# Softmax bands of a local-attention stage moved by DMA instead of ScalarE, and the softmax division moved from GpSimd to ScalarE

## The reference

```
shift_tokens(x):  second half of the features is taken from the token before
q, k, v = split(shift_tokens(x) @ Wqkv)            # 16 heads of 64
q, k = rotary(l2norm(q) * q_scale), rotary(l2norm(k) * k_scale)
# windows of 32 tokens; a token of window w sees windows w-1 and w, through a mask
attn = softmax(8 * q k^T);  x = x + (attn v) @ Wo
h = shift_tokens(x);  h = layernorm(h) * g + b
x = x + (a * gelu(gate)) @ W2 + b2     where a, gate = split(h @ W1 + b1)
```

## Time and profile before

| | us |
|---|---|
| three runs, median (lowest to highest) | 7142.1 (7134.1 to 7146.59) |
| the profiled execution, its own time | 7146.77 |
| its span, first to last instruction | 7144.5 |
| last stage, first to last division L1575 | 3055.2 to 7043.7 |

### The profile page before, as it was taken

How to read it: one execution, slowest core, us unless ns; L and a number is a source line. 1 busy time by engine, 2 the same in 40 slices (tenths; PEclk the granted TensorE clock), 3 DMA queues, 4 the chain that set the end, 5 groups by cost and what they waited for, 6 DMA issues and landing times. The chain is left out here.

```text
span 7144.5 us, 148393 instructions
## 1 busy us (share of the span) xinstructions
PE 5401.0 (76%) x55030; PEld 3273.5 (46%) x55030; DVE 4401.4 (62%) x5698; ACT 3887.7 (54%) x6333; POOL 3429.4 (48%) x1391
## 2 busy tenths in 40 slices
PE   4736777087594848578888888888888888888886
PEld 3524444022121212255555555555555555555554
DVE  4352111342333424488888888888888888888885
ACT  0002222022131213278888777887778778888884
POOL 0000000000000000188888888888888888888883
PEclk8658888588796869789999999999999999999997
DMA  0000000300101010000000000000000000000001
GB/s 17 0 7 20 27 27 27 50 2 12 16 0 27 1 27 0 35 22 7 6 7 28 6 6 13 21 7 6 12 22 7 6 27 6 7 7 12 7 7 28
DMA packets 79753, 102.01 MB, mean 14 GB/s; under 512 B 16344, under 2 KB 55138, under 8 KB 77934
## 3 DMA queue, kind: packets, MB, share of 16 engines
q1 hardware_dynamic: 79632, 100.41, 6.4%
HBM read 63.67 MB, written 11.53 MB: 11 GB/s over the span
## 5 line engine op out<-in xcount | busy, mean ns | idle before, releaser
L99 POOL TENSOR_TENSOR ln_post_rstd<-ln_post_var,neg_half 128x8 f32<-128x8 f32 x16 | 26.6, 1662 | 2922.8 <-DVE ln_post_var L80 2922.8
L1591 POOL TENSOR_TENSOR d_qk_swap<-d_qk_raw,d_rot 128x512 f32<-128x512 f32 x768 | 1389.0, 1838 | 67.4 <-ACT d_qk_raw L1299 40.4
L1598 POOL TENSOR_TENSOR d_rnorm<-d_sq_clip,neg_half 128x32 f32<-128x32 f32 x192 | 1232.4, 6419 | 271.6 <-DVE d_sq_clip L1466 271.6
L834 ACT ACTIVATE c_pt<-c_ps 128x512 f32<-128x512 f32 (+1 forms) x640 | 354.5, 555 | 1118.8 <-PE c_ps L752 1116.8
L1137 PE MATMUL d_ring<-d_wqkv,d_xin 128*128 (+1 forms) x1536 | 810.2, 665 | 174.3 <-ACT d_xin L1389 169.3
L866 DVE TENSOR_REDUCE c_mx<-c_ps 128x1 f32<-128x512 f32 (+3 forms) x768 | 416.8, 556 | 772.9 <-PE c_ps L737 768.9
L1449 DVE TENSOR_TENSOR d_qk_part<-d_qk_raw,d_rot 128x1024 f32<-128x1024 f32 x384 | 597.7, 1559 | 253.6 <-ACT d_qk_raw L1299 251.0
L1575 POOL TENSOR_TENSOR d_probs_n<-d_probs,d_prec 128x1024 f32<-128x1024 f32 x192 | 545.5, 2841 | 315.8 <-DVE d_prec L1491 315.8
L1299 ACT ACTIVATE d_qk_raw<-d_ring 128x512 f32<-128x512 f32 x768 | 435.8, 594 | 453.9 <-PE d_ring L1137 450.2
L766 PE MATMUL c_ps<-c_pt,c_vg 128*32 128x512 f32 (+3 forms) x1536 | 629.3, 507 | 4.7 <-DVE c_ots L871 4.7
L1137 PEld LDWEIGHTS d_ring<-d_wqkv,d_xin 128*128 128x128 f32 x1536 | 319.7, 216 | 560.0 <-issue 449.2
(11 more groups left out here) (259 smaller groups left out, 10498.5 us busy)
## 6 DMA issues: line engine op xcount, KB each, us to landing
d_v_prev<-d_v SPq DMA_DIRECT2D x192, 128.0 KB, 2.3
b_w<-in_L_ffn_w SPq DMA_DIRECT2D x64, 256.0 KB, 3.4
d_wqkv<-in_L_ffn_Wqkv SPq DMA_DIRECT2D x6, 1536.0 KB, 8.7
c_kp<-c_k_scratch SPq DMA_DIRECT2D x30, 256.0 KB
c_qp<-c_q_scratch SPq DMA_DIRECT2D x24, 256.0 KB
d_rot<-in_rot_base SPq DMA_DIRECT2D x6, 1024.0 KB, 6.4
c_k_scratch<-c_kparts SPq DMA_DIRECT2D x5, 768.0 KB, 5.2
c_q_scratch<-c_qparts SPq DMA_DIRECT2D x4, 768.0 KB, 3.6
```

What stands on the lines that cost most here:

```text
L1591: mm = eng.tensor_tensor(qk_swap[:, which, :, out:out + hd], qk_raw[:, which, :, src:src + hd], rot[:, bass.ds(par, 1), which, 1, bass.ds( ...
L1598: eng.tensor_tensor(rnorm[:, :], sq_clip[:, :], neg_half[:, 0:2 * HEADS], ALU.pow).then_inc(rn_ready, 1)
```

## The change

Five edits, all in the last stage.

1. The eight band copies go from ScalarE to SyncE's DMA queue: eight `dma_start` a slot, each 32 partitions x 512 numbers. The band tile becomes 128 x 4 windows x 16 heads x 32, so that each transfer writes one run per partition; the product with v reads it with a stride. `band_ready` counts 16 for each transfer, 128 a slot.
2. SyncE's slot now waits for `blocks_ready`, issues the eight transfers, then waits for `pv_ready` and issues the carry of `v_prev`.
3. The division of the probabilities goes from one GpSimd instruction to sixteen ScalarE instructions of 128 x 64, one per head, with the reciprocal as a scale operand read from `prec`.
4. Order on VectorE: the block transposes stand after the layer-norm and residual steps; in odd slots the row sums and reciprocal stand behind the scaling by the norms. Order on TensorE: `qk(2)` and `qk(3)` go ahead of the W2 product, `values` ahead of the variance product.
5. Order on ScalarE: the input copy `xin` goes ahead of the v copies; in even slots Gelu goes ahead of Exp, behind a one-column Gelu (`table_probe`).

```diff
-        band = [sb(f"band{p}", [P, HEADS, P]) for p in range(2)]
+        band = [sb(f"band{p}", [P, 4, HEADS, WIN]) for p in range(2)]
...
-                    eng.wait_ge(v_evac, 2 * (m + 1))
-                    eng.wait_ge(pv_ready, m + 1)
-                    eng.dma_start(v_prev[P - WIN:P, :], v_sb[p][P - WIN:P, :]).then_inc(v_carried, 16)
+                def slot(n, u, f, g):
+                    if f:
+                        eng.wait_ge(blocks_ready, n - 1)
+                        eng.sem_inc(passed, 1)
+                        if f == 2:
+                            eng.wait_ge(pv_ready, n - 3)
+                        for w in range(4):
+                            r = slice(32 * w, 32 * w + 32)
+                            eng.dma_start(band[u][r, w, :, :], own_t[r, :, :]).then_inc(band_ready, 16)
+                            to = band[u][32 * w - 32:32 * w, w, :, :] if w else band_prev[u][96:128, :, :]
+                            eng.dma_start(to, prev_t[r, :, :]).then_inc(band_ready, 16)
+                    if g:
+                        eng.wait_ge(pv_ready, n - 2)
+                        eng.dma_start(v_prev[P - WIN:P, :], v_sb[1 - u][P - WIN:P, :]).then_inc(v_carried, 16)
...
-                    if u == 0:
-                        if f:
-                            bands((0, 1))
+                    if f:
+                        eng.wait_ge(rec_ready, n - 1)
                         if g:
-                            attended()
-                        if f:
-                            bands((2, 3))
-                    elif f:
-                        bands((0, 1, 2, 3))
+                            eng.wait_ge(blocks_ready, n - 2)
+                        for h in range(HEADS):
+                            mm = eng.activation(probs_n[:, h, :], probs[:, h, :], ACT.Copy, scale=prec[:, h:h + 1])
+                        mm.then_inc(pn_ready, 1)
+                    if g and u == 0:
+                        attended()
...
-                    if f:
-                        eng.wait_ge(rec_ready, n - 1)
-                        if live(3):
-                            eng.wait_ge(blocks_ready, n - 2)
-                        eng.tensor_tensor(probs_n[:], probs[:], prec[:, :].unsqueeze(2).broadcast_to((P, HEADS, 2 * WIN)),
-                                          ALU.mult).then_inc(pn_ready, 1)
```

More of the change, by code:

```diff
@@ L1066, in _, with pairs, through @@
                 eng.wait_ge(zeroed, 1)
-                def carry(m, p):
-                    eng.wait_ge(v_evac, 2 * (m + 1))
-                    eng.wait_ge(pv_ready, m + 1)
-                    eng.dma_start(v_prev[P - WIN:P, :], v_sb[p][P - WIN:P, :]).then_inc(v_carried, 16)
-                def tiles(lo, hi, l):
+                def slot(n, u, f, g):
[12 more added lines that the diff above has]
+                        eng.dma_start(v_prev[P - WIN:P, :], v_sb[1 - u][P - WIN:P, :]).then_inc(v_carried, 16)
+                def pairs(lo, hi, l):
                     with eng.Fori(lo, hi) as k:
                         for u in range(2):
-                            carry(l * NT + k * 2 + u, u)
-                def turn_over(l):
+                            slot(l * NT + k * 2 + u, u, 2, True)
+                for n in range(4):
+                    slot(n, n % 2, int(n >= 2), n >= 3)
+                load(1, 1)
+                pairs(2, 16, 0)
+                def through(l, more):
+                    pairs(0, 2, l)
                     eng.wait_ge(wo_ready, (NT // 2) * l)
                     load_wo(l)
+                    pairs(2, 3, l)
                     eng.wait_ge(w1_ready, 3 * (NT // 2) * l)
@@ L1086, in turn_over @@
                     load_w2(l)
-                tiles(0, 3, 0)
-                load(1, 1)
-                tiles(3, 16, 0)
+                    if more:
+                        eng.wait_ge(x2_ready, (NT // 2) * l)
+                        load(l + 1, (l + 1) % 2)
+                    pairs(3, 16, l)
                 with eng.Fori(1, LAYERS - 1) as l:
[L1092 to L1101, removed]
+                    through(l, True)
+                through(LAYERS - 1, False)
+                slot(TILES, 0, 2, True)
+                slot(TILES + 1, 1, 2, True)
+                eng.wait_ge(v_carried, 16 * (TILES - 1))
                 for b in range(BATCH):
@@ L1179, in attended @@
                     def attended():
-                        eng.wait_ge(band_ready, n - 2)
+                        eng.wait_ge(band_ready, 128 * (n - 2))
                         eng.wait_ge(ot_ready, n - 3)
@@ L1189, in attended @@
                             r, at = place(h)
-                            eng.matmul(op[r:r + 64, h // 2, :], v_sb[1 - p][:, h * DH:(h + 1) * DH], band[1 - p][:, at, :],
+                            eng.matmul(op[r:r + 64, h // 2, :].rearrange("p (w t) -> p w t", t=WIN), v_sb[1 - p][:, h * DH:(h + 1) * DH], band[1 - p][:, :, at, :],
                                        start=(h % 8 < 2), stop=False, skip_group_check=True, tile_position=(0, r))
@@ L1203, in slot @@
                         qk(1)
+                    if a:
+                        qk(2)
+                        qk(3)
                     if late:
@@ L1209, in slot @@
                         mm.then_inc(w2_ready, 1)
-                    if a:
-                        qk(2)
-                        qk(3)
                     if s:
@@ L1238, in slot @@
                         attended()
+                    if s:
+                        par_v = eng.snap(parity(n - 1))
+                        values(0)
+                        values(1)
                     if odd:
@@ L1244, in slot @@
                         mm.then_inc(var_done, 1)
[L1245 to L1248, removed]
                     if even:
@@ L1316, in turned @@
                         eng.activation((qt[:, :, :], kt[:, :, WIN:])[c % 2][:, 4 * half:4 * half + 4, :], src, ACT.Copy).then_inc(t_evac, 1)
[L1318 to L1332, removed]
                     def attended():
@@ L1344, in values @@
                     def values():
+                        eng.wait_ge(v_ready, 2 * n)
+                        if live(-1):
+                            eng.activation(xin[1 - p][:, :], xs[:, bass.ds(eng.snap(column(n + 1)), P)], ACT.Copy).then_inc(xin_ready, 1)
                         for c in range(2):
@@ L1387, in slot @@
                         values()
-                    if live(-1):
+                    elif live(-1):
                         eng.activation(xin[1 - p][:, :], xs[:, bass.ds(eng.snap(column(n + 1)), P)], ACT.Copy).then_inc(xin_ready, 1)
-                    if s and u == 0:
-                        exponent()
                     if even:
+                        eng.activation(table_probe[:, :], keep[:, 0:1], ACT.Gelu)
                         par_f = eng.snap(parity(n - 6))
@@ L1397, in slot @@
                                            bias=b1[0:w, bass.ds(par_f, 1), 3 + c:4 + c].rearrange("p l c -> p (l c)")).then_inc(gelu_ready, 1)
+                    if s and u == 0:
+                        exponent()
                 run(eng, slot, layer_start)
@@ L1484, in slot, with total @@
                         par, i = eng.snap(parity(n)), eng.snap(n % TB)
-                    if f:
+                    def total():
                         eng.wait_ge(exp_ready, n - 1)
@@ L1491, in slot @@
                         eng.reciprocal(prec[:], psum_row[:]).then_inc(rec_ready, 1)
+                    if f and u == 0:
+                        total()
                     if late:
@@ L1505, in slot @@
                                           ALU.mult).then_inc(rope_ready, 1)
+                    if f and u == 1:
+                        total()
                     if a:
@@ L1517, in slot @@
                         cosine(1).then_inc(cos_done, 1)
-                    if f:
-                        blocks()
                     if even:
@@ L1535, in slot @@
                         mm.then_inc(x1_ready, 1)
+                    if f:
+                        blocks()
                     if u == 0 and a:
```

## The result

The changed kernel takes 7913.94 us (median of four runs, 7908.4 to 7919.42) against 7144.35 for the kernel before: ratio 1.1078, 95% interval 1.1059 to 1.1098. That is 770 us slower. The forecast was 7680, the range 7400 to 8010.

A forecast was written before the change was run, and what follows sets the result against it. A loop of waits round all engines bounds the kernel at 41.76 us a pair; the new carry loop takes 45.3 + 0.7 + 1.2 + 0.2 = 47.4, times 95.5 pairs 535 us more: 7680 us, range 7400 to 8010.

The forecast's parts named there:

- The chain named in the prediction: Last stage: loop through transposes, blocks_ready, eight issues, carry, v copies, qk(1), squares and divisions; 46.0 us a pair against 41.76.
- Issues: SyncE: eight band issues ahead of the carry at 0.51 us each, 4.1 us a slot, bounds 0.47 and 0.61.
- TensorE's clock: TensorE idles before qk(1); slow clock adds 0.8 us for qk(3) in odd slots, 0.4 for qk(1) in even.
- Divisions: ScalarE: sixteen divisions at 0.26 us each take 4.2 us a slot, against 5.1 for the bands they replace.
- Odd half: Loop from an odd slot's start, landed carry to landed carry: 25.6 us, against 19.7 from an even slot's.
- the 0.7 that the sum had added for hand-overs: About ten hand-overs between engines outside the listed pieces, each under 0.1 us, add 0.7 us a pair.
- Terms at nothing: Product with v: the strided band read moves the same columns and costs nothing; even doubled, it lies beside ScalarE's carry wait.
- The removed division: GpSimd loses 192 divisions, median 3.73 us; not in the new loop, so this buys nothing there.
- The cheap case: Rival: issues at 0.47, divisions at 0.24, W2 at full clock, no dip; 43.7 us a pair, 7330 us; chance 0.12.
- the dear one: Rival: divisions without overlap (0.36), issues at 0.61, landing at 3 us; 7985 to about 8100 us; chance 0.2.
- the case of hidden transfers: Rival: transfers hidden, issues below 0.16 us, freed GpSimd decides; 39.0 us a pair, 6880 us; chance 0.05.

## Why the prediction was right, and what of it was off

The direction, the mechanism and its place were right. The chain named in the prediction is the one in the trace, and the runs that move the carry or put eight transfers ahead of it show that the issues ahead of the carry cause the loss. The forecast of 535 us was 235 too small, 49.9 us a pair against 47.4. By the terms of the sum:

- **Issues.** Taken as 8 x 0.51 from the carry's own issue. In a row they are 0.63 apart, 5.06 us: 1.9 a pair more. That step was mis-sized, and the measured value lies just outside its stated bounds (0.47 to 0.61). The row taken was of an issue that stands alone, and the rows of issues in a row were of the stage's start, where they take 0.43. One issue in 63 takes 1 to 1.9 us, under 0.1 a slot in the mean; what it waits for was not found.
- **TensorE's clock.** Taken as 0.4 for `qk(1)` in the even slot. There `qk(1)`, `qk(2)` and `qk(3)` all run at the lower level. The copy that reads `qk(1)` starts 5040.05 - 5037.94 = 2.1 us after the product, 1.15 in the sum, and from it to the end of the squares pass 6.9 us where the sum had 5.4, since the fourth copy waits 1.11 for `qk(3)`. That is 2.4 us in place of 0.4. I had taken it for one product because I had looked only at which product waits, not at which follow it. No run held the clock up, but the even halves in which it rose a microsecond earlier were 1.1 us shorter, so about half of the 2.4 us is tied to the clock by the trace. For the rest it is argued.
- **Divisions.** 4.2 a slot forecast, 3.93 measured: 0.5 a pair less. Each takes 349 ns (348 forecast), and they start (3.93 - 0.35) / 15 = 0.24 apart. The rule of the Trainium skill ("ScalarE: Activation LUTs", What ACT_TABLE_LOAD costs) gives 0.24, nearer than my 0.26.
- **Odd half.** From Gelu's table load to the first q/k copy and from there to the transposed ones, 5061.03 to 5065.88 and on to 5071.25 is 10.2 us, 10.4 with the clock's 0.8 in the sum. Right.
- **Why the errors make only 2.5.** Issues and clock are 1.9 and 2.0 a pair above the sum. From the last division to the first transfer pass 1.63 and 1.56 us in the median where the sum had 1.43, 0.3 a pair. Against them stand 0.5 for the divisions, 0.2 to 0.3 in the odd half, and the 0.7 that the sum had added for hand-overs, which the measured pieces already hold. So part of the nearness of 7680 is terms that offset each other.
- **Terms at nothing.** The strided read of the band was taken at nothing: the product with v takes 277 ns a matmul, 278 before.
- **The removed division.** The prediction said that it buys nothing on the new loop. On that loop the move costs 137 us, 3.9 us of sixteen divisions a slot being on it. How much of a single division on GpSimd would be on it was not measured.

The cheap case fell (issues are dearer, not cheaper), the dear one supplied part of the difference by its price of an issue, and the case of hidden transfers is what the run with the carry first makes true: 6904, near the 6880 that was given for it. Its condition was put wrongly, as a price of an issue under 0.16 us; the place in the queue does it at 0.63. That the times are near is no proof of how 6880 was made up (half of GpSimd's two divisions coming back), which no run took apart; in that run VectorE is the fullest engine.

## What to carry to other kernels

When transfers are added to a queue, ask for each one already there what it waits behind now, and write the urgent one first: a transfer that something waits for, put behind eight that nobody reads, cost 10% in the kernel before. In the changed kernel, moving it ahead turned a loss of 10.8% into a gain of 3.4%. Price issues by issues in a row, not by one that stands alone. An order edit is worth only what the next loop leaves: the order edits alone took away the 302 us of waiting in front of W2, but GpSimd then waited longer for the reciprocal, and the kernel got 2.1% slower.

## What the runs showed of the hardware

A transfer issued alone on SyncE holds it for 0.51 us; in a row of eight most take 0.59 and start 0.63 apart, at 64 KB each. The extra transfers of 16 KB are issued at the same pace, eight in 5.0 us, so it doesn't go by their bytes:

```profile
5016.82 4.94 SPq L1078 DMA_DIRECT2D d_extra<-ident  x8
5021.81 0.59 SPq L1079 DMA_DIRECT2D d_v_prev<-d_v  x1
```

Sixteen ACTIVATEs of 128 x 64 with a scale operand, each 349 ns, start 0.24 apart, while band copies of 32 partitions in a row, which they replaced, did not overlap (624 ns each, starts 0.64 apart, as at 5030.29 and 5030.93 us in the trace of before).
